# A selective scan's state buffer: a column wider, kept in scan order, and the gate released by the scan

## The reference, cut to what matters

```python
def step(h, inp):
    u_t, d_t, b_t, c_t = inp
    dA = jnp.exp(d_t[..., None] * A[None])
    h = dA * h + (d_t * u_t)[..., None] * b_t[:, :, None, :]
    y = jnp.einsum('bkdn,bkn->bkd', h, c_t)
    return (h, y)
```

## Time and profile before

| | us |
|---|---|
| median of three runs | 38452.89 (38447.9 to 38454.71) |
| the profiled execution | 38402.84 |
| its span, first to last instruction | 38401.1 |
| VectorE, GpSimd, TensorE, ScalarE busy | 34558.5, 32818.9, 27194.9, 18333.0 |

### The profile page before, as it was taken

One profiled execution on the slowest core, in us unless ns is written; L12 is line 12 of the kernel. 1 busy time (PEld: TensorE's weight loads), 2 busy tenths in 40 slices (PEclk: granted clock), 3 DMA queues, 4 the chain that ended last, 5 costly groups with the idle time before them and its releaser, 6 DMA issues. The chain is left out here.

```text
span 38401.1 us, 329722 instructions
## 1 busy us (share of the span) xinstructions
PE 27194.9 (71%) x75104; PEld 7272.2 (19%) x75104; DVE 34558.5 (90%) x19050; ACT 18333.0 (48%) x22658; POOL 32818.9 (85%) x7776
## 2 busy tenths in 40 slices
PE   5777777777766777777777766777777777766777
PEld 2111111111112111111111112111111111112114
DVE  6999999999977999999999977999999999976993
ACT  4555555555534554545555534555555555534551
POOL 1999999999972999999999962999999999974994
PEclk7777777777777777777777778777777777777775
DMA  4666666666675666666666665666666666676665
GB/s 150 162 159 162 159 161 160 161 159 159 160 227 173 159 159 159 160 159 158 159 160 160 159 219 176 162 160 158 159 160 160 159 162 159 160 224 185 160 160 174
DMA packets 2388440, 6378.07 MB, mean 166 GB/s; under 512 B 691536, under 2 KB 836304, under 8 KB 2376400
## 3 DMA queue, kind: packets, MB, share of 16 engines
q1 hardware_dynamic: 2386640, 6362.76, 63.8%
HBM read 2961.86 MB, written 764.47 MB: 97 GB/s over the span
## 5 line engine op out<-in xcount | busy, mean ns | idle before, releaser
L1252 POOL TENSOR_TENSOR h<-h,c 128x2048 f32<-128x2048 f32 x4992 | 22507.8, 4525 | 1236.6 <-ACT state L1111 1234.2
L1053 DVE TENSOR_TENSOR_SCAN h<-decay,state,slot 128x1024 f32<-128x1024 f32 x6656 | 15615.8, 2346 | 717.5 <-ACT state L1199 38.3
L961 PE MATMUL psy<-h,t_fold 128*32 128x512 f32 x40000 | 12158.1, 783 | 265.7 <-ACT ybuf L1172 265.7
L896 PE MATMUL slot<-bc,pick 96*128 96x512 bf16 x13328 | 5068.1, 477 | 8872.2 <-DVE h L1049 5586.0
L1029 DVE TENSOR_TENSOR slot<-du,slot 128x1024 f32<-128x1024 f32 x6656 | 8050.2, 1209 | 968.7 <-PE slot L896 897.5
L1103 ACT ACTIVATE decay<-delta,na 128x1024 f32<-128x1024 f32 x6664 | 7577.8, 1146 | 2387.9 <-DVE h L1053 2145.4
L1049 DVE TENSOR_TENSOR_SCAN h<-slot,state,made 128x1024 f32<-128x1024 f32 x3328 | 7625.9, 2326 | 18.3 <-ACT slot L1103 18.3
L1272 POOL TENSOR_TENSOR made<-du,b 128x2048 f32<-128x2048 f32 x1664 | 7524.9, 4522 | 128.1 <-DMA b<-bcdram 123.2
L1103 ACT ACTIVATE slot<-delta,na 128x1024 f32<-128x1024 f32 x3328 | 3716.5, 1117 | 6470.8 <-DVE h L1053 6467.4
L961 PEld LDWEIGHTS psy<-h,t_fold 128*32 128x32 f32 x40000 | 2238.1, 131 | 8505.3 <-issue 8200.2
L1264 POOL TENSOR_TENSOR du<-delta,u 128x1024 f32<-128x1024 f32 x628 | 1482.8, 2361 | 2659.3 <-ACT delta L1150 2659.3
(11 more groups left out here) (108 smaller groups left out, 17711.0 us busy)
## 6 DMA issues: line engine op xcount, KB each, us to landing
delta<-delta SPq DMA_DIRECT2D x10048, 128.0 KB, 2.8
du<-du SPq DMA_DIRECT2D x10048, 128.0 KB, 2.9
c<-bcdram SPq DMA_DIRECT2D x6720, 128.0 KB, 2.8
b<-bcdram SPq DMA_DIRECT2D x6688, 128.0 KB, 3.0
u<-useq SPq DMA_DIRECT2D x212, 1536.0 KB, 6.6
yseq<-ybuf SPq DMA_DIRECT2D x624, 512.0 KB, 3.0
ya<-yseq SPq DMA_DIRECT2D x420, 512.0 KB, 4.5
yb<-yseq SPq DMA_DIRECT2D x360, 512.0 KB, 5.4
```

Source lines behind the costliest of these rows:

```text
L896: mm = pe.matmul(slot[s % 2][:, cols], pick[:, rows_of, :], bc[q % 2][:, cols], start=True, stop=True)
L961: mm = pe.matmul(psy[rows, cols], T["fold"][:, :], h[v % H_RING][:, c, cols], start=(v % QUADS == 0), stop=(v % QUADS == QUADS - 1), skip_ ...
L1053: dve.tensor_tensor_scan(out, decay[s % DECAY_RING][:, order], slot[s % 2][:, order], first, ALU.mult, ALU.add).then_inc(sem["h_ready"], 1)
L1252: pool.tensor_tensor(both[:], both[:], c4[g][:].unsqueeze(1).broadcast_to((P, 2, CH)), ALU.mult)\
```

## The change

The buffers of h get 1025 columns for each of the two scans. The scan writes columns 1 to 1024, always in the order in which it scans, so that the last value is in column 1024 in backward chunks too. The gate reads columns 1 to 1024 and writes 0 to 1023. Column 1024, the state to be saved, is thus never overwritten by the gate, and the gate waits for `h_ready` of the unit's second scan instead of `state_saved`. c is read in reverse in backward chunks. psy is then in scan order, and `copy_y` turns it round in backward tiles. What may now overwrite the column is the scan that has the buffer next, four units later: VectorE waits for `state_saved` of the unit four before, and ScalarE gives that semaphore a start of H_RING = 4.

```diff
-        h = ring("h", H_RING, (P, 2, CH))
+        h = ring("h", H_RING, (P, 2, CH + 1))
...
                         dve.wait_ge(sem["reduced"], C0 * UNITS + (v + 1 + REDUCE_LAG))
+
+                        dve.wait_ge(sem["state_saved"], C0 * UNITS + (v + 1))
...
-                    out = h[v % H_RING][:, s % 2, order]
+                    out = h[v % H_RING][:, s % 2, 1:]
...
-                    act.copy(state[:, q if both_ways else 0, k:k + 2], h[v % H_RING][:, :, 0 if backward(q) else CH - 1])\
+                    act.copy(state[:, q if both_ways else 0, k:k + 2], h[v % H_RING][:, :, CH])\
...
-                    act.copy(ybuf[:], psy[:]).then_inc(sem["y_copied"], 1)
...
+                    order = slice(None, None, -1) if backward(q) else slice(None)
+                    act.copy(ybuf[:], psy[:, order]).then_inc(sem["y_copied"], 1)
...
+                act.sem_inc(sem["state_saved"], H_RING)
...
-                    pool.wait_ge(sem["state_saved"], C0 * UNITS + (v + 2))
+                    pool.wait_ge(sem["h_ready"], C0 * STEPS + (2 * v + 2 + H_START))
...
-                    pool.tensor_tensor(both[:], both[:], c4[g][:].unsqueeze(1).broadcast_to((P, 2, CH)), ALU.mult)\
+                    order = slice(None, None, -1) if backward(v // UNITS) else slice(None)
+                    pool.tensor_tensor(both[:, :, 0:CH], both[:, :, 1:],
+                                       c4[g][:, order].unsqueeze(1).broadcast_to((P, 2, CH)), ALU.mult)\
                         .then_inc(sem["gated"], 1)
```

More of the change, by code:

```diff
@@ L1164, in last_part, with copy_y @@
                     act.copy(split[:, 2, :], psc[:, 0:FLAT]).then_inc(sem["split_lo"], 1)
-                def copy_y(C0, T_):
+                def copy_y(C0, T_, q):
                     act.wait_ge(sem["reduced"], C0 * UNITS + (T_ * TILE_UNITS + H_RING + REDUCE_LAG))
                     act.wait_ge(sem["y_stored"], C0 * (16 * TILES) + 16 * (T_ + 1))
-                    act.copy(ybuf[:], psy[:]).then_inc(sem["y_copied"], 1)
-                act.sem_inc(sem["state_saved"], 1)
+                    order = slice(None, None, -1) if backward(q) else slice(None)
+                    act.copy(ybuf[:], psy[:, order]).then_inc(sem["y_copied"], 1)
+                act.sem_inc(sem["state_saved"], H_RING)
                 act.sem_inc(sem["y_stored"], 32)
@@ L1197, in _ @@
                     act.wait_ge(sem["h_ready"], g * (per_g * BS) + H_START)
-                    act.wait_ge(sem["state_saved"], g * (per_g * BU) + 1)
+                    act.wait_ge(sem["state_saved"], g * (per_g * BU) + H_RING)
                     act.copy(state[:].rearrange("p a k -> p (a k)"), T["zeros"][:, :]).then_inc(sem["state_zeroed"], 1)
@@ L1213, in _ @@
                             if n == COPY_Y_AT:
-                                copy_y(C0, s // NS)
+                                copy_y(C0, s // NS, (s // NS - 1) // TILES % BODY_CHUNKS)
                             if (t, n) in SAVE_AT:
@@ L1236, in _ @@
                         save(C0, BU - 1)
-                copy_y(NC, 0)
+                copy_y(NC, 0, BODY_CHUNKS - 1)
             @block.gpsimd
```

## The result

The changed kernel is **slower**: 38666.74 us in the median (38658.46 to 38671.45, five runs) against 38452.89 us of the kernel before in the same comparison (38422.39 to 38469.68, five runs). That is 214 us more. The ratio is 1.0056, with a 95% interval of 1.0042 to 1.0071. The forecast was 38440, a gain too small to measure, in a range up to 38600. The time lies 67 us above that range.

A forecast was written before the change was run, and what follows sets the result against it. VectorE was taken to set the pace, stalled a little by TensorE. From the profiled 38402.8 us, du took off 13 and all else 0, giving 38390; the median lies 50 us higher, so 38440 us, range 38.22 to 38.60 ms.

The forecast's parts named there:

- the scan's wait: VectorE's scan waiting for the state's copy of four units before: it cannot bind, and two added register instructions cost nothing.
- Rival B: Earlier gates shift TensorE's gaps and clock: 38.37 to 38.57 ms; chance 0.12 on the quick side, 0.11 on the slow.
- The bound from the stages: First and second scan stages, same instructions, differ by 62.0 us, 0.6%; taken as how much the clock's pattern can do.
- the copy of y: ScalarE's 288 reversed copies out of PSUM in backward tiles: priced at nothing, at most 52 us.
- VectorE sets the pace, TensorE stalls it a little, and GpSimd follows: Scan stages: VectorE and GpSimd each 95% busy in the first, but no row shows VectorE waiting for GpSimd.
- The gate's release: GpSimd's gates no longer wait 1234.2 us for ScalarE's copy: worth 0 to 374.9 us of span, taken as 0.
- rival A: TensorE's waits for gates hold up broadcasts VectorE needs: up to 375 us go, 38.08 ms; chance 0.12.
- Rival D: GpSimd is busy until ScalarE has copied, no gate starts earlier: 38.45 ms; chance within the forecast's 0.58.
- The du term: du on GpSimd behind the gate moves up: half of VectorE's 26.6 us wait for it saved, 13 us.
- wrong at the root: Sign named beforehand that would refute the forecast: the scan showing a wait for the state's copy.
- The gate: GpSimd's multiplication, reading one word off and c in reverse: no change from about 4.52 us, at most 0.82 us more.
- rival C: The gate gets dearer and GpSimd sets the pace: 39.8 ms for backward gates alone, 41.3 for all; chance 0.07.

The follow-up runs named there:

- e1: The changed kernel without VectorE's wait for the saved state (state_saved) ahead of the scan: 38424.35 us, 0.9997 of the kernel before.
- e5: The changed kernel with VectorE's wait for state_saved moved from the scan to ahead of the product of the same step: 38425.71 us, 0.9992.
- e3: e1 with the gate waiting for ScalarE's copy of the state again, as before the change: 38411.06 us, 0.9994.
- e2: The kernel before with only the scan's wait for state_saved of four units before added: 38702.87 us, 1.0067.
- e4: The kernel before with buffers of h of 1025 columns, the last never used, no shift, all waits as before: 38435.92 us, 1.0000.
- e6: e2 with the added wait in the first chunk of each loop body only: 38457.0 us, 1.0002 of the kernel before.
- e9: e2 with each broadcast issued twice at three steps around each start of a tile: 38337.56 us, 0.9971 of the kernel before.
- e7: e2 with a fourth, always met wait on the opening scan, for VectorE's own earlier scan: 38437.49 us, 0.9996 of the kernel before.
- e13: The kernel before with each broadcast issued twice at three steps around each start of a tile, no added wait: 38290.65 us, 0.9958.
- e12: e5 with every broadcast issued twice: 39011.33 us, 1.0147 of the kernel before.

## Why the prediction was wrong

**The step that failed** is the one on the scan's wait: "Two register instructions come in, in a body of 96 scans, and lie under running ones. Price nothing." Its first half held. The condition is always met, since the decay stands in ScalarE's queue behind the copy, and no row shows the scan waiting for it. But I priced the waiting and the new instructions, and not the third semaphore on an instruction that was there already. (The count was short too: the changed kernel ran 1872 instructions more, 18 a body, two of them register instructions and 16 waits ahead of scans that take GpSimd's product. These lay under running work.) The order shown ahead of the prediction had it in plain sight: [waits b_multiplied,state_saved,reduced]. This costs 29 ns behind the product on the engine that sets the pace, 90.5 us over 3120 scans, a term that should have stood in the sum. The trace of before had both prices, 21 ns at L1052 and 50 ns at L545, and I read neither. With this term alone the sum would have been 38530, inside the range. What carried the time past 38600 is what TensorE's clock made of the delay, the other part of the 214 us.

**Rival B was the right mechanism with the wrong cause and size.** It made the clock's pattern a matter of luck, worth 120 us at the slow end, set off by earlier gates. Early gates set off nothing (e1 and e5 against e3). The longer step from product to scan did, and the slot wait grew by 165 us in the changed kernel and by 217 in e2 (1114.3 - 897.5), in the profiled executions. With the direct part it goes past the range. The bound from the stages, whose steps all had the same length, showed how the pattern varies from start to start, and not how it answers to a longer body. The range was also a little short of its own terms: B's 38.57 ms and 52 us for the copy of y make 38.62.

**What was right.** "VectorE sets the pace, TensorE stalls it a little, and GpSimd follows": GpSimd lost 1676 us of work and nothing of it reached the span. The gate's release is worth nothing (e3 against e1), and rival A is out: TensorE's waits for gates nearly doubled in e3 at no cost. The stall's cause was read rightly as well: TensorE's queue at the low clock. Rival D is out, since no gate waits for ScalarE any more. The du term of 13 us can't be seen in totals that agree to 0.1%, and cannot be credited: VectorE's wait for du is gone in the changed kernel and in e1, but it is down to 0.4 us in e2 too, whose gates are those of before. The scan's odd start, TensorE's rows of 1025 and the reversed copy of y cost nothing: the scan is at 2347 ns, eight matmuls of the reduction take 1.91 us at the full clock as before, and the copy's median is 991 ns at L1177. I wrote that I would be wrong at the root if the scan showed a wait for the state's copy. It shows none, and I was wrong all the same; that list lacked a longer step.

**The gate** was priced at no change, and rival C at dearer. It is cheaper, 4176 ns, in both directions. GpSimd's busy time in a forward and then in a backward chunk of the changed kernel, 24 gates each:

```profile
4917.00:5072.00 155.00, 100.16 (x24) 0.79 0.64 159
5074.00:5229.00 155.00, 100.05 (x24) 0.79 0.65 160
```

That is 4.17 us a gate with c read forward and with c read in reverse. By this the trace agrees with the rule that the prediction takes from the Trainium skill, "GPSIMD Engine Reference", section 7, that reads slow down only from steps of more than 8 bytes: a step of 4 bytes backward costs nothing. No row explains the gain of 0.35 us. e4 shows that it needs the shift and not the wider rows.

**What stays open.** Why the shift shortens the gate was not tried further. Why a delay in the second chunk slows the tile starts more than one in the first is not settled, nor why the first scan of a body waits less in e6. That TensorE's longer pause lowered the clock is shown in one place only; what is shown over the whole kernel is that the projections at the tile starts became slower. And some 28 us of the scan gap in the changed kernel, e2 and e9 stand at four fixed steps (44, 92, 6 and 54), about 0.35 us more each time, steps 44 and 92 in the second layer's stage only and steps 6 and 54 in the last's, which is not in e1 or e5. The scan that opens a body waits some 25 us less in sum, so the two nearly cancel.

## What to carry to other kernels

On the engine that sets the pace, count the semaphores on the instruction right behind the one that it depends on: there a third one cost 29 ns, even when it had long been met. Look for a wait instruction that asks for two semaphores in the trace that you have: its price may stand there already. Put a wait that is always met on an instruction whose asking lies under running work, here the product, where it cost nothing. And where a second engine's clock depends on its pauses, price a small periodic delay at more than its own length: here 90 us became 214, and 270 with the wait alone.

## What the runs showed of the hardware that I had not expected

- A wait instruction of VectorE took 21 ns when it asked for one semaphore and 50 ns when it asked for two (before, e1, e3, e5, e7 against the changed kernel, e2, e9; and within the kernel before, L1052 against L545). In the kernel before the same step was from 17 to 43 ns on GpSimd (L1263) and from 17 to 38 on ScalarE (L1149).
- A multiplication on GpSimd of 128 x 2048 elements took 4176 ns when it wrote one fp32 word below where it read, and 4525 ns when it wrote where it read; 4533 with two rows in that way (e4), and 4526 for the product that it wrote into another buffer.
- TensorE doing more made the kernel faster: 2512 matmuls more at the tile starts (75104 to 77616) gained 0.42% (e13). With all broadcasts doubled, at 88432 matmuls, the time was 1.5% above that of the kernel before (e12).
